# Scaling three turns deep, DMA transposes for the shared activations, accumulates moved, gathers one add sooner

## The chip, the cores and the metric

One core of a Trainium2 chip runs the whole program in one launch. The metric is the device time in microseconds, as the median of several runs. TensorE (PE) multiplies, VectorE (DVE), ScalarE (ACT) and GpSimd (POOL) do the rest, SyncE (SP) only issues DMAs and waits; GpSimd issues the indirect DMAs.

## What is computed

Two layers on `x` (16 sequences of 128 rows, 512 wide). The first is a recurrence over time (WKV) on the normalized rows and a context; the second is a mixture of eight experts, two chosen for each row, beside one shared expert:

```
x = x + wkv(w, u, layernorm(x), ctx)
h = layernorm(x)                                   # 2048 rows of 512
p = softmax(h @ gate_w.T); comb = its two largest  # 8 experts
moe = sum_e comb[:, e] * (silu(h @ eg[e].T) * (h @ eu[e].T)) @ ed[e].T      # inner size 256
sh  = (silu(h @ sg.T) * (h @ su.T)) @ sd.T         # inner size 1024
x = x + moe + sigmoid(h @ seg.T) * sh
```

## The kernel before

**Tiles.** The 2048 rows are 16 tiles of 128. The fp32 operands are split in two fp16 parts, high and low, and each product takes three matmuls (high by high, high by low, low by high). A *unit* is 256 inner columns of one tile: 12 matmuls of 512 columns into `GU` (gate and up, one of two PSUM banks), and 6 into `DN` (down). The shared expert has four units for each tile, 64 in all (`N_EXP`); behind them come 39 slots (`NSLOT`), each one unit of a gathered tile of 128 rows for one routed expert, the last slots being padding.

**One unit, n.** PE fills `GU`. ACT takes the tanh of the gate half into `th` (`unit_tanh`, L654). DVE (`hidden`) makes `th` (L1192) and then the fp32 product `hb` (L1195), and raises `h_rdy`. PE transposes `hb` in two 128x128 pieces into the PSUM bank `HT` (`hidden_t`, L829). ACT copies the high part as fp16 to `hx` (`unit_hi`, L659), DVE the low part (`hidden_lo`, L1200). Two units later PE multiplies `hx` with the down weights (`down_products`, L899). The four units of a tile add up in `DN`, which DVE adds to the tile in `accumulate` (L1206); SP stores it (`store_sum`). The order within PE's unit is: six GU matmuls, the down products of unit n - 2, HT of unit n - 1, six GU matmuls.

**Turns.** The program is written out by hand, engine by engine; each engine runs its list in order and waits on semaphores. Turn i (i = 2 to 15) does the recurrence of tile i (DVE: two scans L1061 and L1064, `add_now` L1071 which raises `nd`, four `reciprocals` L1078; ACT: `both_exps`; POOL: `first_product` L421, `second_product` L424, `quotient` L429 and L432, which gives `yb`), the residual and second norm of tile i - 1 (PE: YT from `yb`, L829; POOL: `norm`, L411 to L415; ACT: `second_norm`, `xnb`, L620; PE: XT), the routing of tile i - 2 and the four shared units of tile j = i - 2. `first_stats(i + 2)` on DVE reads the tile x(i + 2), which SP loads with `load_x`. Turns 0 and 1 have no units. After turn 15 come the last two shared tiles, while lists of rows for each expert are put together, and then the slots.

**Weights.** Each routed expert's weights are loaded (SP), squared and summed for a scale (ACT L599 in `expert_square`, PE L869 and L870 in `sum_squares`, DVE in `small_steps`, POOL in `scales`), and split: ACT makes the high parts (`expert_piece`, L702) and scaled copies (L705), POOL the low parts (`expert_lo`, L445). `SQUARED_IN` says in which turn each expert is squared; `turns` hands each engine `sq_e` (squared in this turn), `hi_e` (high parts, a turn later), `ws_e` and `lo_e`. POOL splits the shared down weights in L494.

**Slots.** POOL gathers slot j's rows (`gather_tile`, L574) into one of six buffers and adds the results with an accumulating indirect DMA (`add_rows`, L584). An add waits for `may_add`, which SP raises when the adds of earlier experts have landed; padding slots wait for all real ones. Gather 5 also waits until the last shared tile is stored.

## Time and profile before

| | us |
|---|---|
| median of 3 runs | 565.74 |
| lowest, highest | 565.31, 566.1 |
| the profiled execution | 566.06 |
| its span | 564.3 |
| granted TensorE clock, share of full speed | 0.985 |

The span runs from the first instruction to the last; the time of the execution has 1.8 us more around it. Busy times are sums of instruction durations; neighbours overlap a little, so a start-to-start distance says more than a duration. A number in brackets behind a timeline row is the idle time of the engine just before it, with what ended it.

### The profile page before, as it was taken

Reading aid. Unit: us, or ns where it says so; the run is one execution under the profiler, and the core shown is the slowest. Engines: PE = TensorE matmul, PEld = TensorE weight load, DVE = VectorE, ACT = ScalarE, POOL = GpSimd, SP = SyncE. Lnnn points to the kernel's source line nnn. Section 1 sums busy time; section 2 is a strip of 40 time slices with the busy share of each in tenths; the row PEclk is TensorE's granted clock in tenths of the full one; section 3 lists DMA queues with packets and bytes.
Section 4 is the critical chain, followed back from the end, with each engine's and each line's share of the span. In section 5 each row is a group of like instructions: output and inputs, shape, how many; then the busy total and the mean of one; then the engine's idle time right before and its main releaser. Section 6 shows DMA issues by size and latency. Waiting matters only on the chain.

```text
span 564.3 us, 10142 instructions
## 1 busy us (share of the span) xinstructions
PE 486.2 (86%) x2671; PEld 258.5 (46%) x2671; DVE 421.3 (75%) x954; ACT 275.9 (49%) x534; POOL 345.4 (61%) x422
## 2 busy tenths in 40 slices
PE   1116789899999999999999979999999999999970
PEld 1113345345455555454555435445545555555530
DVE  5678987899989899999898867566656656666650
ACT  4848837575573864765837333433333333333310
POOL 5767956857948669588486364334375565555332
PEclk9999989999999999999999999999999999999995
DMA  7970105105213223151101320315576776677453
GB/s 283 415 271 19 38 19 187 57 21 188 76 46 143 77 82 143 38 188 62 52 20 39 105 88 15 113 45 102 101 122 117 141 119 116 110 131 123 69 73 38
DMA packets 25929, 59.14 MB, mean 105 GB/s; under 512 B 6314, under 2 KB 6314, under 8 KB 24338
## 3 DMA queue, kind: packets, MB, share of 16 engines
q0 software_dynamic: 9824, 20.90, 21.3%
...
q14 instruction: 31, 0.25, 0.2%
...
## 4 chain that ended last, share of the span: by engine, by line
PE 52%; POOL 17%; issue 10%; DVE 9%; DMA 7%; ACT 3%; SPq 1%; POOLq 0%; DVEq 0%; ACTq 0%
PE GU L884 28%; PE DN L899 14%; DMA out<-wall,idsa 5%; POOL wall L445 4%; PE XT L829 3%; PE HT L829 3%; POOL yb L429 2%; POOL nrm L411 2%; POOL nrm L413 2%; DVE wall L1071 2%; POOL wall L424 2%; POOL wall L421 2%; DVE wall L1078 1%; PE YT L829 1%; SPq L366 1%
## 5 line engine op out<-in xcount | busy, mean ns | idle before, releaser
L884 PE MATMUL GU<-wall,xt 128*128 128x512 f16 x768 | 187.0, 384 | 2.1 <-DVE wall L1173 2.0
L899 PE MATMUL DN<-wall,hx 128*128 128x512 f16 (+1 forms) x618 | 150.8, 380 | 7.2 <-DVE hx L1200 4.5
L884 PEld LDWEIGHTS GU<-wall,xt 128*128 128x128 f16 x768 | 74.8, 99 | 70.4 <-issue 3.7
L584 POOL DMA_INDIRECT out<-wall,idsa x39 | 62.0, 1590 | 73.1 <-SPq L370 35.1
L659 ACT ACTIVATE hx<-HT 128x256 f16<-128x256 f32 x103 | 39.0, 379 | 127.4 <-PE HT L829 110.6
L899 PEld LDWEIGHTS DN<-wall,hx 128*128 128x128 f16 x618 | 60.4, 98 | 81.9 <-issue 6.0
L1200 DVE TENSOR_TENSOR hx<-HT,hx 128x256 f16<-128x256 f32 x103 | 43.1, 418 | 64.3 <-ACT hx L659 59.7
L654 ACT ACTIVATE th<-GU,scl 128x256 f32<-128x256 f32 x103 | 48.5, 471 | 80.0 <-PE GU L884 76.1
L884 PE MATMUL GU<-wall,kb 128*128 x240 | 61.4, 379 | 0.2 <-DVE kb L1374 0.2
L884 PE MATMUL GU<-wall,xnb 128*128 x228 | 58.5, 379 | 0.6 <-DVE xnb L1374 0.6
L574 POOL DMA_INDIRECT xb<-xn_rows,idsi x39 | 40.2, 1030 | 30.5 <-DMA out<-xb 16.3
L1078 DVE RECIPROCAL wall<-wall 128x128 f32<-128x128 f32 x64 | 57.7, 928 | 0.0
L1192 DVE SCALAR_TENSOR_TENSOR th<-th,GU 128x256 f32<-128x256 f32 x103 | 41.5, 403 | 20.5 <-ACT th L654 20.2
L1195 DVE SCALAR_TENSOR_TENSOR hb<-th,scl,GU 128x256 f32<-128x256 f32 x103 | 49.5, 481 | 9.6 <-DVE th L1192 4.8
L445 POOL TENSOR_TENSOR wall<-wall 128x1024 f16<-128x1024 f32 x21 | 44.9, 2141 | 5.4 <-ACT wall L705 3.5
L488 POOL DMA_INDIRECT lists<-toki,posi x32 | 35.4, 1107 | 13.2 <-issue 6.2
L829 PE MATMUL HT<-ident,hb 128*128 128x128 f32 x206 | 40.1, 276 | 3.3 <-DVE hb L1195 3.2
L411 POOL TENSOR_SCALAR nrm<-mv 128x1 f32<-128x1 f32 x32 | 14.1, 442 | 46.2 <-DVE mv L1086 44.7
L829 PEld LDWEIGHTS HT<-ident,hb 128*128 128x128 f32 x206 | 27.9, 141 | 26.5 <-DVE hb L1195 9.4
L1428 DVE TENSOR_SCALAR wall<-DN,scl,wsl 128x512 f32<-128x512 f32 x39 | 31.3, 802 | 2.9 <-PE DN L899 2.8
L884 PEld LDWEIGHTS GU<-wall,kb 128*128 128x128 f16 x240 | 23.5, 98 | 19.9 <-issue 0.7
L829 PE MATMUL KT<-ident,kb 128*128 128x128 f32 x64 | 11.6, 309 | 23.0 <-POOL toki L395 7.8
...
## 6 DMA issues: line engine op xcount, KB each, us to landing
...
out<-xb SPq DMA_DIRECT2D x20, 256.0 KB
xb<-x SPq DMA_DIRECT2D x16, 256.0 KB, 2.7
cb<-ctx_t SPq DMA_DIRECT2D x16, 256.0 KB
xn_rows<-xnb SPq DMA_DIRECT2D x16, 256.0 KB
xb<-xn_rows,idsi POOLq DMA_INDIRECT x39
out<-wall,idsa POOLq DMA_INDIRECT x39
```

What stands on the lines that cost most here:

```text
L445: ins = nc.gpsimd.tensor_tensor(lo, span(wall, raw, GUW // 2), hi, ALU.subtract)
L574: pool.indirect_dma_start(xg[r], None, xn_dram, bass.IndirectOffsetOnAxis(ap=idsi[:, j:j + 1], axis=0)).then_inc(gather[r], 16)
L584: pool.indirect_dma_start(out, bass.IndirectOffsetOnAxis(ap=idsa[:, j:j + 1], axis=0), ye[j % RESULTS], None, compute_op=ALU.add).then_inc ...
L654: nc.scalar.activation(th[par][:], GU[par][:, 0:IE], ACT.Tanh, scale=scale(row, TANH)).then_inc(tanh, 1)
L659: nc.scalar.activation(hx[par][:, 0:IE], HT[:, 0:IE], ACT.Copy).then_inc(h_hi, 1)
L829: ins = nc.tensor.transpose(dst[:, c * P:(c + 1) * P], src[:, c * P:(c + 1) * P], ident[:])
L884: ins = nc.tensor.matmul(GU[par][:], lhs(xp, c), gate_up(base, wp, c), start=m == 0, stop=m == 3 * HC - 1)
L899: ins = nc.tensor.matmul(DN[:], hx[par][:, hp * IE + c * P:hp * IE + (c + 1) * P], down(base, wp, c), start=start and m == 0, stop=stop an ...
L1078: nc.vector.reciprocal(a, a).then_inc(rcp, 1)
L1192: STT(th[par][:], th[par][:], 1.0, GU[par][:, 0:IE], ALU.add, ALU.mult).then_inc(a1, 1)
L1195: STT(hb[par][:], th[par][:], scale(row, KAPPA), GU[par][:, IE:2 * IE], ALU.mult, ALU.mult).then_inc(h_rdy, 1)
L1200: TT(hx[par][:, IE:2 * IE], HT[:, 0:IE], hx[par][:, 0:IE], ALU.subtract).then_inc(h_lo, 1)
```

## The change

- The constant `HX = 3`: three buffers `hx`, and the down products of unit n are issued in unit n + 3 instead of n + 2.
- For the shared units `hb` isn't transposed by PE any more. `unit_hi` and `hidden_lo` write the fp16 parts untransposed to `hr` (two buffers), and SP transposes `hr` into `hx` with one DMA (`turn_hidden`, 128x512 fp16, 128 KB, 64 of them). Every other `hb` now lies in PSUM (bank `HB`, in place of `HT`). For the slots PE still transposes, into `YT`.
- `accumulate`, `hidden_lo`, `unit_hi` and `expert_square` stand elsewhere in the lists; `load_x(i + 3)` at a turn's end becomes `load_x(i + 2)` near its start; `store_sum` is last in a turn.
- Experts are squared in the even turns 2 to 14 instead of 2, 3, 5, ..., 13, and expert 0's squares, sums and scales go into turns 2 and 3. One matmul of four columns takes the place of two of two columns. All experts get the three steps of splitting in three turns.
- An expert's weights are loaded in six DMAs of 256 KB between the transposes, instead of one of 1024 KB and one of 512 KB.
- After the turns the second norm comes ahead of expert 6's low parts on POOL, and two of these behind the read of the lists.
- Gather j is issued ahead of add j - 7 instead of behind it.

The core of the diff (in order: names, SP, POOL in turn 3, POOL after the turns and in the slots, ACT, PE):

```diff
+HX = 3
+PIECES = 6
-SQUARED_IN = [2] + list(range(3, 2 * E - 2, 2))
+SQUARED_IN = list(range(2, 2 * E, 2))
...
-        HT, DN = bank("HT"), bank("DN")
+        HB, DN = bank("HB"), bank("DN")
+        hb = [HB[:, 0:IE], hb1[:, :]]
+        hb_routed = [by_time[:, 0:IE], hb1[:, :]]
...
+            def turn_hidden(n):
+                sp.wait_ge(h_lo, n + 1)
+                wait_from(sp, dn, n - HX + 1)
+                sp.dma_start(hx[n % HX][:, :].rearrange("p (c t) -> p c t", t=P), hr[n % 2][:],
+                             transpose=True).then_inc(h_turned[n % HX], 16)
...
             def turn(i, j, sq_e, hi_e, ws_e, lo_e):
...
+                if j > 0:
+                    turn_hidden(n - 1)
...
+                if i > LAG + 1 and i + 2 < B:
+                    load_x(i + 2)
+                if i < B - 1:
+                    load_ctx(i + 1)
+                piece(0)
+                turn_hidden(n)
+                piece(1)
+                turn_hidden(n + 1)
+                store_xn(i - 1)
+                piece(2)
+                turn_hidden(n + 2)
+                if j > 0:
+                    store_sum(j - 1)
...
+                if i == LAG + 1:
+                    scales(2, 0)
...
-            expert_lo(E - 2, 1)
-            expert_lo(E - 2, 2)
             norm(B - 1, 1, agg2, norm2, xn_rdy)
+            expert_lo(E - 2, 0)
...
+            expert_lo(E - 2, 1)
+            expert_lo(E - 2, 2)
             scales(E + 1, E - 1)
...
                 gather_tile(j)
-                add_rows(j - GATHERS)
+                if j > GATHERS:
+                    add_rows(j - GATHERS - 1)
...
             def unit_hi(n, par):        
-                act.wait_ge(h_t, n + 1)
-                wait_from(act, dn, n - 1)
-                nc.scalar.activation(hx[par][:, 0:IE], HT[:, 0:IE], ACT.Copy).then_inc(h_hi, 1)
+                act.wait_ge(h_rdy, n + 1)
+                if n >= 2:
+                    act.wait_ge(h_turned[(n - 2) % HX], 16 * ((n - 2) // HX + 1))
+                nc.scalar.activation(hr[par][:, 0:IE], hb[par], ACT.Copy).then_inc(h_hi, 1)
...
                 second_norm(i - 1)
+                unit_hi(n + 1, 1)
...
                 if i + 1 < B:
                     both_exps(i + 1)
-                unit_hi(n + 1, 1)
...
                 if before is not None:
-                    down_products(n - 2, par, *before)
-                if not (isinstance(n, int) and n == 0):
-                    hidden_t(n - 1, 1 - par)
+                    down_products(n - HX, *before)
+                if n > N_EXP:
+                    hidden_t(n - 1)
...
-            down_products(n - 2, n % 2, base_of[NSLOT - 2], True, True, B + NSLOT - 2)
-            hidden_t(n - 1, (n - 1) % 2)
-            down_products(n - 1, (n - 1) % 2, base_of[NSLOT - 1], True, True, B + NSLOT - 1)
+            hidden_t(N_EXP + NSLOT - 1)
+            for j in range(NSLOT - HX, NSLOT):
+                down_products(N_EXP + j, base_of[j], True, True, B + j)
```

VectorE in one turn, before, from the low part of unit n - 1 (the previous tile's last) to `hidden` of unit n + 2:

```order
277 L1200 TENSOR_TENSOR hx<-HT,hx 128x256
278 L1071 TENSOR_TENSOR wall<-wall 128x8x127
...
286 L1081 BN_STATS st<-xb 128x6
287 L1086 BN_AGGR mv<-st 128x2
288 L1200 TENSOR_TENSOR hx<-HT,hx 128x256
289 L1206 SCALAR_TENSOR_TENSOR xb<-DN,gate,xb 128x512
290 L1078 RECIPROCAL wall<-wall 128x128
...
294 L1078 RECIPROCAL wall<-wall 128x128 x2
295 L1200 TENSOR_TENSOR hx<-HT,hx 128x256
296 L1078 RECIPROCAL wall<-wall 128x128
```

and the same place afterwards (L1263 is `hidden_lo`, L1131 `add_now`, L1269 `accumulate`, L1138 a reciprocal, L1141 the statistics):

```order
320 L1263 TENSOR_TENSOR hr<-hb,hr 128x256
321 L1131 TENSOR_TENSOR wall<-wall 128x8x127
...
329 L1263 TENSOR_TENSOR hr<-HB,hr 128x256
330 L1141 BN_STATS st<-xb 128x6
331 L1146 BN_AGGR mv<-st 128x2
332 L1138 RECIPROCAL wall<-wall 128x128
...
336 L1138 RECIPROCAL wall<-wall 128x128
337 L1269 SCALAR_TENSOR_TENSOR xb<-DN,gate,xb 128x512
338 L1138 RECIPROCAL wall<-wall 128x128
339 L1263 TENSOR_TENSOR hr<-hb,hr 128x256
340 L1138 RECIPROCAL wall<-wall 128x128
```

The low part of unit n moved ahead of the statistics of the next x, and the accumulate moved from there to between the reciprocals, behind `hidden` of unit n + 1.

SP in one turn with weights, before (L275 `load_x`, L280 `load_ctx`, L284 `store_xn`, L290 `store_sum`):

```order
56 L280 DMA cb<-ctx_t 128x512
57 L305 DMA wall<-wgu 128x2048
58 L306 DMA wall<-wd 128x1024
59 L284 DMA xn_rows<-xnb 128x512
60 L290 DMA out<-xb 128x512
```

and afterwards (L282 `load_x`, L320 `turn_hidden`, L314 a piece of weights):

```order
60 L320 DMA_TRANSPOSE hx<-hr 128x4x128
61 L282 DMA xb<-x 128x512
62 L287 DMA cb<-ctx_t 128x512
63 L314 DMA wall<-wgu 128x512
64 L320 DMA_TRANSPOSE hx<-hr 128x4x128
65 L314 DMA wall<-wgu 128x512
66 L320 DMA_TRANSPOSE hx<-hr 128x4x128
67 L291 DMA xn_rows<-xnb 128x512
68 L314 DMA wall<-wgu 128x512
69 L320 DMA_TRANSPOSE hx<-hr 128x4x128
70 L297 DMA out<-xb 128x512
```

Four transposing DMAs stand between SP's others, each behind a wait for its own unit's low part; the load of x is ahead of the reading turn's other transfers and behind one of them.

## Rows read from the trace of the kernel before

**Rows 1.** The page: busy us (share of the span), instructions of each engine.
```profile
PE 486.2 (86%) x2671; PEld 258.5 (46%) x2671; DVE 421.3 (75%) x954; ACT 275.9 (49%) x534; POOL 345.4 (61%) x422
```
**Rows 2.** Busy time by stretch; columns in the header, counts in brackets.
```profile
core 0: us, PE busy (x) PEld busy (x) DVE busy (x) ACT busy (x) POOL busy (x), PEclk, DMA share, GB/s
...
73.00:318.00 245.00, 237.75 (x1372) 125.47 (x1370) 221.30 (x515) 149.81 (x301) 171.78 (x231) 0.99 0.25 85
...
363.00:543.00 180.00, 177.68 (x934) 95.95 (x932) 110.48 (x234) 56.11 (x116) 92.60 (x70) 1.00 0.60 105
```
**Rows 3.** The same view of one pair of turns.
```profile
199.23:237.02 37.79, 36.95 (x217) 19.88 (x216) 35.24 (x83) 23.84 (x48) 27.88 (x37) 1.00 0.27 98
```
**Rows 4.** Timeline of TensorE in that pair: start, duration, instruction.
```profile
207.99 0.38 PE L829 MATMUL HT<-ident,hb 128*128 128x128 f32 x2
208.21 1.46 PE L884 MATMUL GU<-wall,xt 128*128 128x512 f16 x6
...
228.68 0.66 PE L829 MATMUL YT<-ident,yb 128*128 128x128 f32 x4 [0.84 <-POOL yb L432]
```
**Rows 5.** Timeline of VectorE in the same pair.
```profile
213.36 0.42 DVE L1200 TENSOR_TENSOR hx<-HT,hx 128x256 f16<-128x256 f32 x1
213.70 1.21 DVE L1071 TENSOR_TENSOR wall<-wall 128x1016 f32<-128x1016 f32 x1
...
217.51 0.67 DVE L1081 BATCH_NORM_STATS2 st<-xb 128x6 f32<-128x512 f32 x1
...
223.97 0.42 DVE L1200 TENSOR_TENSOR hx<-HT,hx 128x256 f16<-128x256 f32 x1 [0.68 <-ACT hx L659]
...
228.61 0.42 DVE L1200 TENSOR_TENSOR hx<-HT,hx 128x256 f16<-128x256 f32 x1
```
**Rows 6.** Timeline of GpSimd in the same pair: the end of its chain.
```profile
228.35 0.27 POOL L432 TENSOR_SCALAR yb<-cb 128x4 f32<-128x4 f32 x1
```
**Rows 7.** Table of DMA issues: KB each, median us to landing.
```profile
xb<-x SPq DMA_DIRECT2D x16, 256.0 KB, 2.7
```
**Rows 8.** Timeline of SP's issues in the same pair.
```profile
205.52 0.33 SPq L275 DMA_DIRECT2D xb<-x  x1
...
210.19 0.42 SPq L306 DMA_DIRECT2D wall<-wd  x1
```
**Rows 9.** Timeline of ScalarE in turn 2.
```profile
55.22 1.04 ACT L599 ACTIVATE junk<-wall 128x1024 bf16<-128x1024 f32 x1
```
**Rows 10.** The chain that ended last, in turn 2: start, us, what.
```profile
66.22 2.04 issue
68.26 1.27 POOL wall L421
```
**Rows 11.** Timeline of TensorE: three of its waits.
```profile
100.34 1.47 PE L899 MATMUL DN<-wall,hx 128*128 128x512 f16 x6 [0.91 <-DVE hx L1200]
...
330.58 0.66 PE L829 MATMUL XT<-ident,xnb 128*128 128x128 f32 x4 [3.19 <-ACT xnb L620]
...
355.91 1.46 PE L899 MATMUL DN<-wall,hx 128*128 128x512 f16 x6 [1.00 <-DVE xb L1206]
```
**Rows 12.** The page's groups: GpSimd's low parts of experts.
```profile
L445 POOL TENSOR_TENSOR wall<-wall 128x1024 f16<-128x1024 f32 x21 | 44.9, 2141 | 5.4 <-ACT wall L705 3.5
```
**Rows 13.** Timeline of GpSimd in the slots: gather 5, add 5, gather 12, adds 36 and 37.
```profile
375.79 2.54 POOL L574 DMA_INDIRECT xb<-xn_rows,idsi  x1 [14.78 <-DMA out<-xb]
...
410.22 1.59 POOL L584 DMA_INDIRECT out<-wall,idsa  x1 [4.59 <-DVE wsl L1439]
412.12 0.99 POOL L574 DMA_INDIRECT xb<-xn_rows,idsi  x1 [0.30 <-SPq L370]
...
544.27 1.56 POOL L584 DMA_INDIRECT out<-wall,idsa  x1 [2.88 <-DVE wall L1428]
552.11 1.56 POOL L584 DMA_INDIRECT out<-wall,idsa  x1 [6.28 <-SPq L370]
```
**Rows 14.** Timeline of VectorE at the end: the result of slot 36, and the last `hb`.
```profile
543.18 0.81 DVE L1428 TENSOR_SCALAR wall<-DN,scl,wsl 128x512 f32<-128x512 f32 x1
...
544.55 0.48 DVE L1195 SCALAR_TENSOR_TENSOR hb<-th,scl,GU 128x256 f32<-128x256 f32 x1 [0.17 <-DVE th L1192]
```

192 lines of the change are left out of this document (112 added, 80 removed).

## The prediction

> **What bounds the kernel now.** I read the page first, then the idle time of TensorE, then one pair of turns on every engine. The page gives TensorE 86% of the span and VectorE 75% [rows 1], an average over five stages; the table by stretch separates two of them [rows 2]. Turns 3 to 15 fill 73 to 318 us: TensorE is busy 237.8 us of 245, but VectorE is busy 221.3. The routed stage, 363 to 543 us, is TensorE's alone (177.7 of 180). Before 73 us ScalarE, VectorE and GpSimd wait for one another in turn 2, and behind the last slot there are transfers and waits.
>
> Two turns repeat with a period of 37.8 us, of which TensorE is busy 36.95 and VectorE 35.24 [rows 3]. So each turn costs 18.9 us, and an engine stands right behind TensorE. What ends TensorE's idle time here is the transpose YT, which waits 0.84 us for GpSimd's `yb` in one turn of two [rows 4]. GpSimd's chain in that turn runs from 214.8 us, where VectorE has made the sums (`nd`) that it waits for, to 228.6 us: two scatters, two products of L445, two norms, two products, the quotient [rows 5, 6]. VectorE waits about 2.0 us in the pair, nearly all of it before three of its eight `hx` rows, for ScalarE; one of them is the 0.68 us at 223.97 [rows 5]. Its work, with the small gaps between instructions, therefore needs about 35.8 us per pair.
>
> **The transposes that go.** Each shared unit loses its two TensorE transposes HT. From one start to the next, two of them take 208.21 - 207.99 = 0.22 us [rows 4]; their busy time of 0.38 overlaps the neighbours. Per pair of turns that is 8 units x 0.22 = 1.76 us. The second sum-of-squares matmul, which takes its place in the stream for as long (0.2 us), goes once per pair, since one matmul of four columns takes the place of both. TensorE's own work is 37.8 - 0.84 = 36.96 us now, so about 35.0 us afterwards.
>
> But GpSimd's chain is untouched by that: from its start to `yb` it keeps its 13.8 us, while the units ahead of YT shrink by three transposes, 0.66 us. The wait of 0.84 becomes 1.5 us in the turn with the two L445 products. TensorE's side of the pair is then 35.0 + 1.5 = 36.5 us.
>
> **VectorE's side.** `hidden_lo` still runs eight times per pair, reading `hb` instead of HT. Its present step is 213.70 - 213.36 = 0.34 us [rows 5]; half of them now read SBUF alone, for which I take off 0.2 us per pair in all. The rest is the same work in another order. The waits for ScalarE that followed HT mostly go, because `unit_hi` starts on `h_rdy` and stands ahead of the four exponentials. So 35.6 us, plus what the change adds: `load_x(i+2)` is now issued in the same turn that reads it, behind `turn_hidden(n-1)`. From the end of `hidden_lo(n-1)` (213.78) to `first_stats(i+2)` (217.51, plus 0.35 for the `hidden_lo` placed ahead) VectorE has 4.1 us; such a load takes 2.7 us from issue to landing [rows 5, 7]. That leaves about 1.3 us for issuing the transposing DMA. A plain DMA occupies SP for 0.33 to 0.42 us [rows 8], the bound below; no row shows the transposing form, and with 2.6 us as the bound above the wait would be 1.3 us per turn. I take 0.3 us, nearer the plain issue: 35.6 + 0.6 = 36.2 us.
>
> The larger side sets the pair: 36.5 us against 37.8, so 1.3 us. In 245 us there are 6.5 pairs: **-8.5 us**, with ends of -18 (TensorE's 35.0 alone) and +3 (VectorE with 1.3 us a turn: 35.6 + 2.6 = 38.2).
>
> **The turned activations.** The 64 DMAs of 128 KB have to land in time. From the end of `hidden_lo` to the down products there are, by units of 4.4 us and a lag of three, 6.7, 5.7, 5.7 and 5.7 us for the four units of a turn: for instance the `hidden_lo` of the third unit stands at 228.61 and ends at 229.0 [rows 5], and its products would come one unit and six GU matmuls behind the YT of 228.68 [rows 4], at about 234.7. The nearest row is a plain transfer of 256 KB with 2.7 us [rows 7]; on the other side stands an accumulating scatter, 544.27 until it releases the next at 552.11, less SP's bookkeeping in between: about 4.8 us [rows 13]. I take 3 to 4.5 us with queueing behind a 256 KB piece, which is under 5.7: cost nothing, cover the two units of matmuls between. Beyond 5.7 us both TensorE (operand) and ScalarE (`hr` is overwritten two units later) wait, and the loop closes over three units, so each us costs a third of a us per unit. SP's other waits in a turn (`xn_rdy`, `dn_free`, `y_rdy`) stand behind the transposing DMA that is due earlier, and those events are past by then.
>
> What the Trainium skill says here, apart from the sum: "VectorE: DVE Perf Modes", section "The three transpose paths", gives 1309 ns for one 128x128 tile by DMA against 390 ns on TensorE and advises TensorE where PSUM will do. Four tiles one after the other would be an estimated 5.2 us by that page of the Trainium skill, at the very edge of the window, which speaks against the change. "Advanced Engine Details and Errata", section "X-Bar Transpose (TRN2)", says instead that transposing DMAs are as fast as others, an estimated 0.4 us of transfer. No run shown here decides between the two; for TensorE the trace gives 0.11 us each in the stream, below the 390 ns of the Trainium skill [rows 4].
>
> **Start.** In turn 2, ScalarE loses the three squares of expert 0 (three of some 1.1 us, the first at 55.22) [rows 9]. GpSimd waited for the exponentials behind them, 66.22 to 68.26 [rows 10], so YT(2) comes 2.0 us sooner; GpSimd's own work up to 66.2 is then next. Turn 3 gains the squares instead: TensorE waits behind unit 1 for the third square, which follows a tanh on ScalarE (0.5 + 1.15 us), +1.7, and `scales(2, 0)` ahead of `first_product(4)` costs YT(3) some 0.6. Expert 0's pieces 4 and 5 leave turn 3 (2 x 1.1 us), where they had pushed `hx` and `hb`: TensorE's wait of 0.91 us at 100.34 [rows 11] and the two of 0.8 us that follow it within six us mostly go, -2.2. Sum **-1.9 us**, ends -5 and +3.
>
> **After the turns.** GpSimd did two L445 products, 2.14 us each [rows 12], ahead of `norm(B - 1)`; TensorE waited 3.19 us for `xnb`, until 330.58 [rows 11]. With the norm first `xnb` can be there up to 4.3 us sooner, before TensorE arrives: -3.2. The wait of 1.00 us at 355.91 for the accumulate goes [rows 11], since that is placed a unit later, with the products it needs: -1.0. HT in eight units is 1.8 us, of which the chain of lists may eat half: -0.8. Here `expert_lo(E-2, 1)` and `(2)` and `scales` follow the read of the lists, 4.3 + 2.6 us on GpSimd, which then idled nearly as long for the lists to come back, so the first gather stays about where it was. Sum **-5.0 us**, ends -6 and -1.
>
> **Routed stage.** Its transposes stay, in YT, so 39 slots keep 4.54 us. The gathers come one slot sooner in the row and the adds one slot later. At its head, `accumulate(B - 1)` moves from slot 1 to 2, and gather 5, which waits for its store (375.79 now) [rows 13], slips by 4.5 us to about 380.3; it lands at the 384 us where unit 4 wants it: +0.7. The wait of 1.3 us for gather 12, queued behind add 5 (410.22, 412.12) [rows 13], goes: -1.3. Sum **-0.5 us**, ends -2 and +3.
>
> **End.** A lag of three leaves `down(36)` behind the last unit. Slot 36's result was written at 543.18 and added at 544.27; the two slots after it wait for that add to land, the next goes at 552.11 [rows 13, 14]. With the change: last `hb` 545.0 [rows 14], HT's two transposes, six matmuls 1.3, the result 0.8, the add issued at 547.6: **+3.3 us**, nothing covers it.
>
> **Sum.** -8.5 - 1.9 - 5.0 - 0.5 + 3.3 = -12.6 us. The profiled execution took 566.06 us around its span of 564.3; the median is 565.74. From 566.06 that gives 553.5, and against the median 553.1. I say **553.2 us**.
>
> **Rivals.** *Late turns, slower.* If the transposing DMA takes over 5.7 us, or occupies SP longer than a unit, every turn pays: 4/3 us per turn for each us of excess, over 16 sets. The gain of 12.6 is used up at an excess of 0.6, landing in 6.3 us; at 7 us the time is 553.2 + 16 x 1.7 = 581. For it: there is no row of its kind, and one in-order queue shared with loads. Against: plain transfers of twice the size land in 2.7. The 1309 ns per tile of the Trainium skill ("VectorE: DVE Perf Modes", "The three transpose paths") would lead here if the issue and a piece of weights came on top; no run shown bears it out. Chance 0.18.
> *VectorE waits for x.* With 1.3 us a turn the turns cost 38.2 us per pair and the gain there turns into +3: 564.5, no change to speak of. For it: the load was a whole turn ahead before. Chance 0.14.
> *TensorE alone.* The GpSimd wait does not grow, for its chain starts sooner with VectorE ahead: 35.0 to 35.4 us per pair, -17: 545. Chance 0.12.
> *As forecast*, 547 to 560: 0.56.
>
> About 0.2%, 1.1 us, is what a measurement of this kernel can tell from no change. Faster holds the forecast, TensorE alone and half of the x rival, 0.75; same 0.06; slower 0.19, the late turns and a little of the x rival. The range takes in the x rival and TensorE alone and leaves out the far half of the late turns: 543 to 569.
>
> **What would show it.** Right: a pair of turns of about 36.5 us, YT waiting 1.5 us for `yb` in one turn of two, no wait before DN for the DMA, no wait before `xnb` at 320 us, and slots of 4.54 us. Wrong: DN or `hr` waiting for the DMA transposes, SP busy over 1.3 us in one, VectorE idle before the statistics of x, or YT without a wait at all.

## The result and the profile after

The kernel after takes 576.19 us (median of four runs, 575.17 to 577.17) against 565.57 us for the kernel before beside it (565.31 to 566.1): a ratio of 1.0181 with a 95% interval of 1.0144 to 1.0217. It is slower by 10.6 us where 12.6 us less were forecast, and lies outside the range. The profiled span is 573.4 us, 9.1 more than before.

The page of the kernel after, to be held against [rows 1]: TensorE is busy 10.1 us less than before and VectorE 8.9 us more; the wait of YT for `yb`, 30.7 us, heads TensorE's idle time.

```profile
PE 476.1 (83%) x2525; PEld 242.0 (42%) x2525; DVE 430.2 (75%) x954; ACT 274.3 (48%) x534; POOL 345.9 (60%) x422
L886 PE MATMUL YT<-ident,yb 128*128 128x128 f32 x64 | 11.8, 314 | 30.7 <-POOL yb L475 30.7
```

Marks on TensorE's timeline (the router products of turns 5 and 15, the transposes of slot 0's gathered tile, the start of the last unit's gate-up products, the end) cut the 9.1 us into pieces. For each I set the forecast beside it; the -8.5 us of the pairs is spread by 1.3 us a pair, since one pair lies ahead of turn 5 and half a pair behind turn 15:

| stretch | before, us | after, us | change | forecast |
|---|---|---|---|---|
| start to turn 5 (119.53, 118.94) | 119.5 | 118.9 | -0.6 | -1.9 and -1.3 |
| ten turns, 5 to 15 | 188.65 | 190.76 | +2.1 | -6.5 |
| turn 15 to the first slot | 53.34 | 57.09 | +3.75 | -5.0 and -0.7 |
| slots | 177.51 | 177.83 | +0.3 | -0.5 |
| end | 25.3 | 28.8 | +3.5 | +3.3 |

**The pair of turns.** The table by stretch for one pair from router to router answers to [rows 3]: the pair is 37.57 us long where it was 37.8; TensorE is busy 35.20 us of it (35.0 forecast), VectorE 35.91 (35.24 before), and VectorE waits 1.1 us besides, 0.47 of it for x.

```profile
196.89:234.46 37.57, 35.20 (x200) 17.54 (x198) 35.91 (x83) 23.54 (x48) 28.05 (x38) 1.00 0.50 129
```

TensorE's timeline, YT alone: first the kernel before, then after. The number in brackets is the wait ahead of it. What TensorE no longer does stands there as waiting: 2.07 + 0.30 us a pair, where it was 0.84.

```profile
190.88 0.66 PE L829 MATMUL YT<-ident,yb 128*128 128x128 f32 x4 [0.84 <-POOL yb L432]
209.50 0.60 PE L829 MATMUL YT<-ident,yb 128*128 128x128 f32 x4
228.68 0.66 PE L829 MATMUL YT<-ident,yb 128*128 128x128 f32 x4 [0.84 <-POOL yb L432]
```
```profile
192.51 0.66 PE L886 MATMUL YT<-ident,yb 128*128 128x128 f32 x4 [0.29 <-POOL yb L475]
212.09 0.66 PE L886 MATMUL YT<-ident,yb 128*128 128x128 f32 x4 [2.07 <-POOL yb L475]
230.08 0.66 PE L886 MATMUL YT<-ident,yb 128*128 128x128 f32 x4 [0.30 <-POOL yb L475]
```

GpSimd in the turn between the first two of these YT, kernel after (other lines left out). From the end of one `yb` (192.45) to the next (212.04) there are 19.6 us, and no bracket in it is above 0.52: scales, two scatters, two low parts of weights (L488), two norms, two products, the quotient, back to back.

```profile
192.22 0.23 POOL L475 TENSOR_SCALAR yb<-cb 128x4 f32<-128x4 f32 x1
...
198.62 1.14 POOL L531 DMA_INDIRECT lists<-toki,posi  x1 [0.52 <-POOL scl L520]
...
201.06 2.13 POOL L488 TENSOR_TENSOR wall<-wall 128x1024 f16<-128x1024 f32 x1
...
204.49 2.13 POOL L488 TENSOR_TENSOR wall<-wall 128x1024 f16<-128x1024 f32 x1
...
211.79 0.25 POOL L475 TENSOR_SCALAR yb<-cb 128x4 f32<-128x4 f32 x1
```

The same turn of the kernel before, from the `yb` at 209.07 to the one at 228.35 [rows 6]. GpSimd has no gap here either; its longest wait is about a third of a us:

```profile
209.07 0.23 POOL L432 TENSOR_SCALAR yb<-cb 128x4 f32<-128x4 f32 x1
...
215.25 1.13 POOL L488 DMA_INDIRECT lists<-toki,posi  x1 [0.29 <-DVE mask L1166]
...
217.66 2.14 POOL L445 TENSOR_TENSOR wall<-wall 128x1024 f16<-128x1024 f32 x1
...
221.09 2.13 POOL L445 TENSOR_TENSOR wall<-wall 128x1024 f16<-128x1024 f32 x1
```

**Behind the turns.** GpSimd, VectorE and TensorE of the kernel after around the read of the lists. GpSimd's two low parts stand where the change put them, behind the read; a 24-element subtract on VectorE that starts 0.20 us ahead of them takes 4.46 us and ends with them (in the kernel before it took 0.18); the cast of the ids stands behind it on VectorE, so TensorE waits 4.39 us, and 12 products behind the wait take 4.45 us where others take 2.75.

```profile
348.35 4.22 POOL L488 TENSOR_TENSOR wall<-wall 128x1024 f16<-128x1024 f32 x2
```
```profile
348.15 4.46 DVE L1372 TENSOR_TENSOR cb<-lga,mxa 128x24 f32<-128x24 f32 x1
...
356.82 0.26 DVE L1470 CAST yb<-by_time 39x128 f32<-39x128 int32 x1
```
```profile
357.13 0.25 PE L1066 MATMUL KT<-ident,yb 39*128 39x39 f32 x1 [4.39 <-DVE yb L1470]
357.32 4.45 PE L940 MATMUL GU<-wall,xt 128*128 128x512 f16 x12
...
362.90 2.75 PE L940 MATMUL GU<-wall,xt 128*128 128x512 f16 x12
```

ScalarE at the end of turn 15: all six pieces of expert 6 stand ahead of the norm `xnb` that TensorE then waits 2.64 us for (3.19 before, [rows 11]). In the kernel before two pieces stood there (2.17 us from 322.91).

```profile
322.97 3.21 ACT L754 ACTIVATE wall<-wall,scl 128x1024 f16<-128x1024 f32 x3
326.09 3.21 ACT L757 ACTIVATE wall<-wall,scl 128x1024 f32<-128x1024 f32 x3
...
329.51 0.80 ACT L665 ACTIVATE xnb<-xb,nrm 128x512 f32<-128x512 f32 x1
```

**The transposing DMAs.** The view of the tile `hx` on SP's queue: 64 issues, each 1.2 us of SP. In this kernel TensorE waited for one of them only: the products 0.2 us, their weight load 0.7. That DMA was issued at 347.42, so it took 3.85 us from the start of its issue to the weight load at 351.27.

```profile
L320 SPq DMA_TRANSPOSE hx<-hr x64: 1189/1196/1601, 58.1 to 372.2; - x64
...
who waited for it (us, times):
  PEld DN L958: 0.7, 1
  PE DN L958: 0.2, 1
```
```profile
351.27 0.33 PEld L958 LDWEIGHTS DN<-wall,hx 128*128 128x128 f16 x3 [0.67 <-DMA hx<-hr]
```

### The profile page after: what moved, and what is told of

Same layout as the page of the kernel before. It is cut to its first block, busy times and chain, and to the rows that moved or that the text cites. A ratio compares the mean times of both kernels' runs of the same rounds, so it can differ in the third digit from the quotient of the medians.

```text
span 573.4 us, 9946 instructions
## 1 busy us (share of the span) xinstructions
PE 476.1 (83%) x2525; PEld 242.0 (42%) x2525; DVE 430.2 (75%) x954; ACT 274.3 (48%) x534; POOL 345.9 (60%) x422
## 2 busy tenths in 40 slices
DMA packets 65353, 67.53 MB, mean 118 GB/s; under 512 B 41642, under 2 KB 41642, under 8 KB 64786
## 4 chain that ended last, share of the span: by engine, by line
PE 37%; POOL 18%; DVE 17%; issue 11%; DMA 7%; ACT 4%; SPq 3%; POOLq 0%; DVEq 0%; ACTq 0%
PE GU L940 21%; PE DN L958 11%; DVE wall L1138 4%; POOL wall L488 3%; PE XT L886 3%; DMA out<-wall,cb 3%; POOL yb L472 2%; PE YT L886 2%; POOL nrm L454 2%; DMA xb<-x 2%; POOL wall L467 2%; POOL nrm L456 2%; DVE st L1141 1%; POOL wall L464 1%; DMA xb<-xn_rows,cb 1%
## 5 line engine op out<-in xcount | busy, mean ns | idle before, releaser
L940 PE MATMUL GU<-wall,xt 128*128 128x512 f16 x768 | 191.6, 392 | 4.5 <-DVE wall L1233 4.5
L628 POOL DMA_INDIRECT out<-wall,cb x39 | 62.0, 1589 | 73.5 <-SPq L413 35.9
L1138 DVE RECIPROCAL wall<-wall 128x128 f32<-128x128 f32 x64 | 59.1, 932 | 0.0
L618 POOL DMA_INDIRECT xb<-xn_rows,cb x39 | 38.6, 989 | 33.8 <-DMA out<-xb 21.5
L1261 DVE TENSOR_TENSOR hx<-YT,hx 128x256 f16<-128x256 f32 x39 | 16.5, 424 | 40.8 <-ACT hx L706 40.8
L488 POOL TENSOR_TENSOR wall<-wall 128x1024 f16<-128x1024 f32 x21 | 44.8, 2135 | 0.2
L706 ACT ACTIVATE hx<-YT 128x256 f16<-128x256 f32 x39 | 14.9, 383 | 61.4 <-PE YT L886 61.4
L886 PE MATMUL YT<-ident,yb 128*128 128x128 f32 x64 | 11.8, 314 | 30.7 <-POOL yb L475 30.7
L1494 DVE TENSOR_SCALAR wall<-DN,scl,cb 128x512 f32<-128x512 f32 x39 | 31.3, 803 | 4.9 <-PE DN L958 4.6
L940 PEld LDWEIGHTS GU<-wall,xnb 128*128 128x128 f16 x228 | 22.3, 98 | 18.8 <-issue 0.7
L1141 DVE BATCH_NORM_STATS2 st<-xb 128x6 f32<-128x512 f32 x32 | 22.1, 692 | 8.1 <-DMA xb<-x 7.5
```

Source lines behind the costliest of these rows:

```text
L488: ins = nc.gpsimd.tensor_tensor(lo, span(wall, raw, GUW // 2), hi, ALU.subtract)
L618: pool.indirect_dma_start(xg[r], None, xn_dram, bass.IndirectOffsetOnAxis(ap=idsi[:, j:j + 1], axis=0)).then_inc(gather[r], 16)
L628: pool.indirect_dma_start(out, bass.IndirectOffsetOnAxis(ap=idsa[:, j:j + 1], axis=0), ye[j % RESULTS], None, compute_op=ALU.add).then_inc ...
L886: ins = nc.tensor.transpose(dst[:, c * P:(c + 1) * P], src[:, c * P:(c + 1) * P], ident[:])
L940: ins = nc.tensor.matmul(GU[par][:], lhs(xp, c), gate_up(base, wp, c), start=m == 0, stop=m == 3 * HC - 1)
L1138: nc.vector.reciprocal(a, a).then_inc(rcp, 1)
```

## The experiments

The theory after this reading (theory A in what follows): in the turns of the kernel after, a loop through GpSimd, with ScalarE and VectorE in it, sets the time, not TensorE; behind the turns, three placements cost time each in its own place. The rivals: TensorE still bounds the pair; the transposing DMAs cost something themselves; VectorE alone bounds.

**1. Give TensorE its work back.** In `unit`, ahead of the products:

```diff
+                if 0 < n <= N_EXP:
+                    for c in range(IC):
+                        nc.tensor.transpose(GU[par][:, c * P:(c + 1) * P], ident[:], ident[:])
                 products(par, lhs, base, 0, 3)
```

> The kernel after, with two 128x128 transposes of the identity ahead of each unit's gate-up products in the turns and the first unit of the slots (64 units), so that TensorE has back about the work that the change took from it (2 x 0.11 to 0.14 us a unit, near 2 us a pair of turns, 15 to 18 us over the whole), while the DMA transposes stay. Results are unchanged. Theory A (in the steady turns TensorE is not the bound; its freed time became the wait for yb): the filling goes into the waits, 0 to +3 us, so 576 to 579 us, and the YT waits shrink from 30.7 us to about 16. Rival (TensorE's own work bounds the pair): +12 to +15 us, 588 to 591. Third: if the shorter idle time gives the clock back, it could even come out 1 to 3 us faster than the kernel after.

Measured: 579.09 us, 1.0233 [1.0198, 1.0268], 2.9 us above the kernel after. The pair is 38.3 us instead of 37.6, though 1.6 us of work went in (TensorE busy 36.81 us for 35.20), so TensorE did not bound it. But it stands close behind: 0.7 of the 1.6 us lengthened the pair, and the waits of YT fell to 24.4 us in all, not to the 16 that theory A gave.

```profile
212.72 0.66 PE L886 MATMUL YT<-ident,yb 128*128 128x128 f32 x4 [1.47 <-POOL yb L475]
```

**2. The moves without the DMAs.** `hb` in SBUF, transposed by TensorE into a bank, `unit_hi` and `hidden_lo` reading the bank; all positions, the distance of three units and the tail as in the kernel after:

```diff
-                if n > N_EXP:
+                if n > 0:
                     hidden_t(n - 1)
-                act.wait_ge(h_rdy, n + 1)
-                nc.scalar.activation(hr[par][:, 0:IE], hb[par], ACT.Copy).then_inc(h_hi, 1)
+                act.wait_ge(h_t, n + 1)
+                nc.scalar.activation(hx[n % HX][:, 0:IE], HB[:, 0:IE], ACT.Copy).then_inc(h_hi, 1)
```

> The kernel after with everything that it moves kept, but the shared units' hidden activations transposed by TensorE into a PSUM bank as before (two 128x128 transposes a unit, behind the down products of unit n-3) and no transposing DMA. It splits the change into the transposes and the moves. Theory A (the moves made the rest of the loss, the DMA transposes gained nothing because TensorE was not the bound): within 2 us of the kernel after, 575 to 579 us. Rival B (the transposing DMAs themselves cost, by queue or memory): it goes back towards 565 to 570. Rival C (the DMA transposes gained their TensorE time and the moves lost far more): 588 and above.

Measured: 576.86 us, 1.0214 [1.0176, 1.0252]; theory A. In the table by stretch (columns as in [rows 3]) its pair is 38.05 us, TensorE busy 36.91, so the DMAs bring 0.5 us of the 1.8 a pair; turn 3 gave that back, for its router stood at 77.0 us here and at 80.5 in the kernel after (run 12 looks at that). From turn 15 to the first slot it is the other way round, 60.5 us here and 57.1 there. With the DMAs or without, the moves cost the 10.6 us.

```profile
192.82:230.87 38.05, 36.91 (x216) 19.65 (x215) 35.25 (x83) 23.88 (x48) 27.66 (x38) 1.00 0.34 98
```

**3. and 4. GpSimd less, VectorE less,** in the kernel after:

```diff
+                if k == 1 and e < E - 2:
+                    nc.gpsimd.memset(lo, 0.0)
+                    return
                 ins = nc.gpsimd.tensor_tensor(lo, span(wall, raw, GUW // 2), hi, ALU.subtract)
```
```diff
-                    nc.vector.reciprocal(a, a).then_inc(rcp, 1)
+                    nc.vector.reciprocal(a[:, 0:T // 2], a[:, 0:T // 2]).then_inc(rcp, 1)
```

> The kernel after with GpSimd's second low-part subtraction of experts 0 to 5 (128x1024, 2.135 us each, one a pair of turns) replaced by a memset of the same half-width region; the routed experts' low parts of that half are left out of the computation, nothing else changes. GpSimd gets 1 to 2 us a pair. Theory A (the pair closes over a loop through GpSimd, ScalarE and VectorE, and GpSimd's share is on it): each pair gets shorter by 1 to 2 us, 5 to 11 us in all, 565 to 571. Rival B (VectorE alone bounds the pair): little, 0 to 2 us. If a memset on GpSimd takes as long as the subtraction, this says nothing.

> The kernel after with the reciprocals (64 of 128x128, 0.932 us each, four a turn) over the first 64 columns only, which leaves half of each quotient's reciprocal out of the computation; VectorE gets about 0.4 us each, 1.7 us a turn, 3.4 us a pair back. Theory A (loop through GpSimd, ScalarE and VectorE, with VectorE's queue on it in the even turn): the pair falls from 37.6 towards TensorE's own 35.0 plus its waits, 1.5 to 2.5 us a pair, 10 to 16 us in all, 560 to 566. Rival (GpSimd alone bounds): 0 to 3 us.

Measured: 569.64 us, 1.0083 [1.0057, 1.0108], and 565.81 us, 0.9995 [0.9978, 1.0011]. The totals look as if VectorE were worth more; the pair says otherwise. GpSimd's 1.17 us less (the memset takes 0.965 us) made the pair 36.53 (190.24 to 226.77), 1.04 us shorter; VectorE's 3.2 us less made it 37.24 (186.90 to 224.14), 0.33 shorter. So nine tenths of what GpSimd lost came off the pair. Of VectorE's it was one tenth, or three tenths of what its busy time lost: that fell by 1.07 us only (34.84 for 35.91), as small operations beside GpSimd's grew longer (the two of 128x16 in a pair from 1.02 to 2.14 us).

Run 4's total doesn't measure VectorE. Of the 9.2 us by which its span is shorter, 2.1 lie ahead of turn 5 and 3.0 in the ten turns. The other 4.1 lie behind the turns, 3.2 of them behind the last down products, where no reciprocal stands and only the waits between the last adds changed. The values left out go into the routing, so the lists of rows can differ; that this is the reason is inferred. First run 3, then run 4:

```profile
190.24 0.66 PE L889 MATMUL YT<-ident,yb 128*128 128x128 f32 x4 [0.29 <-POOL yb L475]
208.84 0.66 PE L889 MATMUL YT<-ident,yb 128*128 128x128 f32 x4 [1.14 <-POOL yb L475]
226.77 0.66 PE L889 MATMUL YT<-ident,yb 128*128 128x128 f32 x4 [0.25 <-POOL yb L475]
```
```profile
206.41 0.66 PE L886 MATMUL YT<-ident,yb 128*128 128x128 f32 x4 [2.05 <-POOL yb L475]
```

**5. The low parts ahead of the read of the lists,** in GpSimd's tail:

```diff
             scatter(B - 4)
-            for t in range(B - 3, B):
+            scatter(B - 3)
+            expert_lo(E - 2, 1)
+            expert_lo(E - 2, 2)
+            for t in range(B - 2, B):
                 scatter(t)
...
-            expert_lo(E - 2, 1)
-            expert_lo(E - 2, 2)
             scales(E + 1, E - 1)
```

> The kernel after with GpSimd's last two low-part subtractions of expert 6 (2 x 2.1 us) back ahead of the read of the lists (between the second and the third of the last four scatters) instead of behind it. Theory A (in the kernel after they run beside VectorE's 24-element subtract at 348.15, which takes 4.46 us until they end, and TensorE then waits 4.39 us for the slots' ids and falls to half clock for 1.7 us more): the 4.46 us subtract falls to 0.2 us, the ids' transpose comes up to 4.4 us sooner and no clock is lost, -4.4 to -6 us, 570 to 572. Rival (the list read itself, now 2 to 4 us later, is what TensorE waits for): 0 to -2 us, and the subtract is short all the same.

Measured: 568.38 us, 1.0053 [1.0033, 1.0073], 7.8 us less than the kernel after: the largest single placement, and more than the 4.4 to 6 expected. By the profiles the span is 7.1 us shorter: 5.9 in the stretch of the edit, turn 15 to the first slot (51.17 for 57.09), and 0.7 in the ten turns, where the edit changes nothing. The subtract is short again, and the wait for the ids and the slow products behind it are gone:

```profile
347.33 0.18 DVE L1373 TENSOR_TENSOR cb<-lga,mxa 128x24 f32<-128x24 f32 x1
```

**6. ScalarE's last pieces out of turn 15,** on top of run 5:

```diff
-                if i == B - 1:
-                    ws_e = hi_e
...
             unit_hi(n, 0)
+            expert_piece(E - 2, 4)
+            expert_piece(E - 2, 5)
             router_out(B - 1)
```

> The same as the one before (GpSimd's two subtractions ahead of the read of the lists), and ScalarE's last two scaled pieces of expert 6 (2 x 1.1 us) out of turn 15, where the change had put them ahead of the norm for which TensorE waits, to behind the first hidden copy that follows the turns. Theory A (TensorE's 2.64 us for xnb at 330.37 is ScalarE's queue of six pieces): the wait falls by 1.6 to 2.6 us and the half clock behind it (1.3 us) goes, -1.6 to -3 us against the run before, 567 to 570. Rival (the norm waits for GpSimd anyway, or the pieces come back as a wait of GpSimd's low parts): 0, and GpSimd's read of the lists later.

Measured: 569.93 us, 1.0085 [1.0052, 1.0118], 1.6 us above run 5 with intervals that overlap: the rival. TensorE's wait for `xnb` halved, from 2.65 to 1.32 us, but a wait of 4.00 us for VectorE's `posi` came in its place. It is the same collision again: a 16-column operation of VectorE on SBUF alone takes 3.84 us until GpSimd's two low parts are done.

```profile
334.60 4.21 POOL L488 TENSOR_TENSOR wall<-wall 128x1024 f16<-128x1024 f32 x2
```
```profile
335.01 3.84 DVE L1198 TENSOR_TENSOR pos<-ones,pos 128x16 f32<-128x16 f32 x1
```
```profile
339.84 0.17 PE L934 MATMUL LG<-mask,tri 128*128 128x8 f16 x1 [4.00 <-DVE posi L1218]
```

**7. The end in the order of before.** On the kernel after:

```diff
+            down_products(N_EXP + NSLOT - HX, base_of[NSLOT - HX], True, True, B + NSLOT - HX)
             hidden_t(N_EXP + NSLOT - 1)
-            for j in range(NSLOT - HX, NSLOT):
+            for j in range(NSLOT - HX + 1, NSLOT):
```

with VectorE's `expert_rows(NSLOT - HX)` likewise ahead of the last `hidden_lo`.

> The kernel after with only the end in the order of before: the third-last slot's down product ahead of the last slot's transposes, and its rows ahead of the last low part, so that its add starts sooner. Theory A (the end is a chain of adds that starts when the third-last slot's rows are ready, and the change pushed that row back by the last transposes and their 1.78 us wait): -2.0 to -3.3 us, 573 to 574. Rival (the adds are bound by the last one's own row): 0.

Measured: 572.96 us, 1.0139 [1.0102, 1.0177]. Of the 3.2 us the trace shows 1.1 at the end (from the last gate-up products at 545.76 to the end of the span, 24.8 us; 26.0 in the kernel after). The rest is in the turns, where this profile lacks the slow groups that the one of the kernel after has at 173.34. The interval overlaps that of the kernel after.

**8. The load of x ahead of the transposing DMA,** in SP's turn:

```diff
+                if i > LAG + 1 and i + 2 < B:
+                    load_x(i + 2)
                 if j > 0:
                     turn_hidden(n - 1)
                 if i == LAG:
                     load_x(i + 3)
-                if i > LAG + 1 and i + 2 < B:
-                    load_x(i + 2)
```

> The kernel after with the load of the turn's rows of x issued by SP ahead of the turn's first transposing DMA instead of behind it. Theory A (VectorE's waits for x, 0.47 us in the odd turns and 2.9 us over all turns, are time at which it holds the loop): -1 to -3 us, 573 to 575. Rival (VectorE makes the wait up because GpSimd is later anyway): within 1 us of 576.

Measured: 573.66 us, 1.0152 [1.0115, 1.0189], 2.5 us less by the medians, but again with overlapping intervals and the same steady pair of 37.6 us. That the load costs anything is not shown.

**9. and 10. The three repairs together (5, 7 and 8), with the DMAs and without** (the latter with the edit of run 2):

> The kernel after with three of the repairs together: GpSimd's two subtractions ahead of the read of the lists, the end in the order of before, and the loads of x ahead of the turn's first transposing DMA. Theory A (the three are independent, since they lie in three stretches): 576.2 - 7.8 - 3.2 - 2.5 = 562.7 us, 561.5 to 564.5, below the kernel before. Rival (a part of each gain was the clock's or a later stage takes it back): 565 to 568.

> The same three repairs, and the shared units' hidden activations transposed by TensorE as before, without the transposing DMAs. It shows what the transposing DMAs are worth when the other moves no longer hide it. Theory A (nothing in the turns, since the pair closes over GpSimd, ScalarE and VectorE; the steady pair was 38.05 us with TensorE's transposes and 37.6 with the DMAs, 2.7 us over six pairs, and turn 2 gave that back): 562 to 565 us, within 1.5 us of the run before. Rival (they are worth their 2.7 us or more now): 565 to 567.

Measured: 565.98 us, 1.0004 [0.9987, 1.0020], and 569.55 us, 1.0057 [1.0036, 1.0078]. The first is 3.3 us above the sum of the parts, as could be said of 7 and 8 above: their medians promised more than their rows. The second is slower by 3.6 us with intervals apart: the transposing DMAs do bring something once the other stretches hide nothing. The profiles, each of the longest execution of its kernel, are 5.1 us apart: 1.2 ahead of turn 5, 0.5 in the ten turns (0.5 a pair, less a slow group of 1.7 that only run 9 has there), 2.5 between turn 15 and the first slot, and 0.9 behind. In run 9 a longer wait stands in the slots: 2.02 us for a gathered tile, with slow products behind it.

```profile
383.54 0.65 PE L887 MATMUL XT<-ident,xb 128*128 128x128 f32 x4 [2.02 <-DMA xb<-xn_rows,cb]
...
385.19 2.63 PE L959 MATMUL DN<-wall,hx 128*128 x6
```

**11. Two units behind in the slots.** On the kernel after with the edits of 5 and 8, the down products at a distance of two in the slots, as before; `accumulate(B - 1)` so comes one slot sooner:

```diff
-                if j == HX - 1:
+                if j == 1:
                     accumulate(B - 1)
-                if j >= HX:
-                    expert_rows(j - HX)
+                if j >= 2:
+                    expert_rows(j - 2)
```

> The kernel after with GpSimd's two subtractions ahead of the read of the lists and the load of x ahead of the transposing DMA (two of the three repairs that gave 566.0 together), and in the slots the down products two units behind instead of three, as before: the last mix tile's accumulate stands one slot sooner, and the end drains two units. Theory A (the three-unit distance holds the last tile's accumulate, store and so the sixth gather back, for which TensorE waits 2.0 us and drops to half clock, and it lengthens the end): 566.0 less 2 to 4 us, 562 to 564. Rival (the end alone matters, and its repair already gave that): 565.5 to 566.5.

Measured: 563.27 us, 0.9958 [0.9943, 0.9974]: 2.1 us less than the kernel before, and 2.7 us less than run 9, intervals apart. VectorE's accumulate moves from 376.03 to 372.41 us (first run 9, then this one), and the gathered tile for which run 9 waited 2.02 us no longer comes late.

```profile
376.03 0.74 DVE L1271 SCALAR_TENSOR_TENSOR xb<-DN,gate,xb 128x512 f32<-128x512 f32 x1
```
```profile
372.41 0.74 DVE L1273 SCALAR_TENSOR_TENSOR xb<-DN,gate,xb 128x512 f32<-128x512 f32 x1
```

**12. VectorE's scans behind `yb` in turn 3,** on the kernel after:

```diff
+                if i == LAG + 1:
+                    dve.wait_ge(y_rdy, i)
                 scan_e(i)
                 scan_ev(i)
```

> The kernel after with one wait added: in turn 3 VectorE's two scans wait for the yb of turn 2. In the kernel after they start at 70.84, beside GpSimd's product of yb at 70.91, which takes 2.23 + 1.02 us there and 1.29 + 0.23 us where nothing runs beside it (the kernel with TensorE's transposes), and one of the scans takes 2.25 us instead of 1.2. Theory A (they hold each other up): the yb product ends 1.7 us sooner, TensorE's wait of 7.16 us falls to 5.4, and turn 3 starts 1 to 1.7 us sooner: 574.5 to 575.2 us. Rival (VectorE, 1.6 us later, gives it back in turn 3): 576.

Measured: 573.87 us, 1.0138 [1.0095, 1.0180], an interval that overlaps that of the kernel after. The rows are clear. In the kernel after `yb` took 2.23 + 1.02 us beside the scans:

```profile
70.91 2.23 POOL L472 TENSOR_TENSOR yb<-wall 128x512 f32<-128x512 f32 x1
73.23 1.02 POOL L475 TENSOR_SCALAR yb<-cb 128x4 f32<-128x4 f32 x1
```

and here, with VectorE held, 1.29 + 0.24; YT comes at 72.37 us and not at 74.31, turn 3's router at 78.96 and not at 80.51:

```profile
70.70 1.29 POOL L472 TENSOR_TENSOR yb<-wall 128x512 f32<-128x512 f32 x1
72.08 0.24 POOL L475 TENSOR_SCALAR yb<-cb 128x4 f32<-128x4 f32 x1
```

**13. and 14. The kernel before, two of the moves alone.** The last norm ahead of expert 6's low parts (these between the scatters, as in run 5) and `accumulate(B - 2)` ahead of its neighbour unit; then the gathers one add sooner as well (GpSimd's part of the first is shown):

```diff
-            expert_lo(E - 2, 1)
-            expert_lo(E - 2, 2)
             norm(B - 1, 1, agg2, norm2, xn_rdy)
             scatter(B - 4)
-            for t in range(B - 3, B):
+            scatter(B - 3)
+            expert_lo(E - 2, 1)
+            expert_lo(E - 2, 2)
+            for t in range(B - 2, B):
                 scatter(t)
```

> The kernel before with two of the change's moves alone: the last turn's norm ahead of GpSimd's last two low parts of expert 6, which then go between the second and the third of the last scatters, and the accumulate of the second-last tile ahead of its neighbour unit. Theory A (before, TensorE waits 3.19 us for xnb at 330.58 and 1.00 us at 355.91 for DN, and both go): -3.2 to -4.2 us, 561.4 to 562.5. Rival (as in the kernel after, ScalarE's queue is next, and the wait shrinks by a fraction): 0 to -1.5 us, 564 to 565.6.

> The same on the kernel before, and the gathers of the slots issued one add sooner. Theory A (TensorE waits about 1.3 us at one slot for a gathered tile): a further -1.0 to -1.5 us. Rival (an issue earlier on one queue pushes the adds back by the same, and the end is the adds'): 0 to +1 us.

Measured: 561.26 us, 0.9926 [0.9898, 0.9953], and 560.75 us, 0.9915 [0.9887, 0.9942], the fastest version here that computes everything, ahead of both kernels. The wait for `xnb` fell from 3.19 us to 0.38 and the one for DN went: without ScalarE's four further pieces in the way the two moves give nearly what the prediction gave them. Turn 15 to the first slot became 2.8 us shorter (50.50 for 53.34). A new wait of 1.48 us for `posi` took part of it back, behind a 128x16 operation of VectorE of 1.55 us that ends with GpSimd's two low parts, the collision of run 6 once more. Of the 5.1 us between the two profiles another 1.5 lies ahead of turn 5, where the edit changes nothing. The gathers alone add 0.5 us, which the intervals don't tell from nothing.

```profile
326.21 0.66 PE L830 MATMUL XT<-ident,xnb 128*128 128x128 f32 x4 [0.38 <-ACT xnb L621]
```

**15. and 16. Did TensorE bound the pair of before?** The edits of 3 and 4, on the kernel before.

> The kernel before with GpSimd's second low-part subtraction of experts 0 to 5 (2.1 us each) replaced by a memset of the same region, so that half's low parts are left out of the computation. In the kernel after the same edit gave GpSimd 1.17 us a pair (2.135 to 0.965) and shortened the pair by 1.05 us (37.6 to 36.5). It asks whether TensorE bounded the pair of before, as the prediction took it. If TensorE does (own work 36.96 of 37.8): the wait for yb of 0.84 us goes at most, 0 to 0.85 us a pair, 0 to -5 us in all, and the pair ends near 37.0. If the loop through GpSimd bounds it already: -1.05 a pair, 36.8, -6.5 us in all.

> The kernel before with the reciprocals over half their columns (half of each quotient left out of the computation): VectorE gets 0.4 us on each of 64, 3.2 us a pair. In the kernel after the same edit moved the steady pair by 0.35 us only, and the whole by 10.4 us, most of it at the start and behind the turns. If TensorE and the loop through GpSimd bound the pair of before: 0 to -0.5 us a pair, and little at the start and the end, where TensorE's own waits are shorter: -2 to -5 us, 561 to 564. If VectorE bounds it: -1 us a pair and more, below 558.

Measured: 566.34 us, 1.0013 [0.9990, 1.0036], and 558.76 us, 0.9898 [0.9857, 0.9940]. Ten turns took 188.7 us before, 188.1 with less GpSimd work (117.7 to 305.8) and 187.9 with less VectorE work (116.2 to 304.1). On the average neither frees the pair. With GpSimd shorter, the wait for `yb` is gone (first row below). In the pair around 207 us the turn that ended in it fell from 19.18 to 18.32 us from YT to YT, by just that wait; the other turn rose from 18.62 to 19.03. With VectorE shorter, three of the five pairs came to 36.7 us, TensorE's own work without idle time, and the other two to 38.9 and 39.0 (the two rows by stretch, columns as in [rows 3], are one of each). So TensorE's own 36.7 to 37.0 us is the floor under the pair, and the other engines stand close behind it. That TensorE alone bounded the pair as it stood is not shown: its one wait was for GpSimd. Run 16's total has the same flaw as run 4's, 3.1 us of it lie in the end.

```profile
207.61 0.66 PE L832 MATMUL YT<-ident,yb 128*128 128x128 f32 x4
```
```profile
116.16:152.83 36.67, 36.67 (x217) 20.04 (x216) 31.61 (x81) 23.50 (x47) 26.46 (x37) 1.00 0.30 102
152.83:191.76 38.93, 37.27 (x217) 19.53 (x216) 33.24 (x84) 24.40 (x50) 28.01 (x37) 1.00 0.28 96
```

**17. and 18. Move GpSimd's work into its idle time.** In both lines, the first two low parts of an expert at the front of the turn in which GpSimd idles for 5 us, and ScalarE's fifth piece a turn sooner. On run 11 with the edit of run 12, and on run 14 (GpSimd's part of the first is shown):

```diff
-                if lo_e is not None:
-                    expert_lo(lo_e, 1)
+                if ws_e is not None:
+                    expert_lo(ws_e, 0)
+                    expert_lo(ws_e, 1)
```

> The kernel with two of the repairs and the two-unit distance in the slots (563.3 us), with the wait ahead of turn 3's scans, and with GpSimd's first two low-part subtractions of an expert (2 x 2.14 us) moved to the front of the even turn, where GpSimd stands idle for 5.0 us before the norm (212.0 to 217.1 in the steady pair); for it ScalarE makes the fifth scaled piece one turn sooner, in a gap of 1.7 us. All work stays. The odd turn, where TensorE waits 2.09 us for yb, has one subtraction instead of two. Theory A (the loop through GpSimd bounds the pair at about one for one, VectorE at a tenth, TensorE's own work is 35.0 to 35.3 us): -1.5 to -2.1 us a pair over six pairs and -1.5 at turn 3, 549 to 553 us. Rival B (VectorE's 35.8 us and ScalarE's latency stand right behind): -0.5 to -1 a pair, 556 to 559. Rival C (nothing, since the work comes back as waits elsewhere): 561 to 563.

> The same move of GpSimd's subtractions, and of ScalarE's fifth piece, on the best version of the kernel before (560.75 us: norm and accumulate sooner, gathers one add sooner). Its difference from the run above is what the transposing DMAs and the change's other moves are worth once GpSimd is off the loop. Theory A (TensorE's own 36.96 us bounds the pair of before, which stands at 37.8): the wait for yb of 0.84 us a pair goes at most, -2 to -5 us, 556 to 559, so the kernel after, so repaired, is the faster by 3 to 8 us. Rival (the pair of before is bound by GpSimd as much): below 555.

Measured: 564.87 us, 0.9974 [0.9959, 0.9989], and 565.61 us, 0.9996 [0.9979, 1.0012]: nothing on the first, 4.9 us lost on the second. The turn that waited 2.07 us for `yb` did become 2.0 us shorter (router to router 196.05 to 213.64, 17.6 us, against 19.6), for the 2.14 us that left it. The other became 2.5 us longer (20.54 against 17.99). I had put the two behind GpSimd's wait for the mask, so that they did not fill the idle time but began at its end and pushed the norm back:

```profile
217.15 4.23 POOL L488 TENSOR_TENSOR wall<-wall 128x1024 f16<-128x1024 f32 x2 [4.43 <-DVE mask L1228]
```

What they give ahead of that wait was not tried, so whether the 549 to 553 us of that expectation can be had stays open.

## Why the prediction was wrong

Two steps failed: the pair of turns, 8.6 us off over the ten turns, and the stretch behind the turns, 9.4 us off.

**The pair, -8.5 us.** TensorE's own work came out as worked out (35.20 us against 35.0). What failed is the sentence that let the wait grow from 0.84 to 1.5 us, "from its start to `yb`" GpSimd "keeps its 13.8 us". It took VectorE's `nd` as the start. The trace names `mask`, and GpSimd hardly waited for it (0.29 us): in the kernel before, too, it worked from the `yb` of one turn (209.30) to that of the next (228.62) almost without a gap, 19.3 us, of the 19.2 from YT to YT. That turn was GpSimd's already. Taking work from TensorE in it could only lengthen the wait; the turn became 19.6. Only the other turn, 18.6 long with no wait, had something to give, and came to 18.0. So 0.2 us a pair, not 1.3. Runs 1, 2, 3 and 15 show it from four sides. On top, the ten turns hold a pair with a group at half clock and a longer first pair, about 1.9 and 0.9 us: that is the +2.1.

VectorE's side was no bound, but its work was misjudged as well: 0.67 us more in the pair, where the step took 0.2 off. The largest part is in small operations beside GpSimd's (the two of `chosen`, 128x2, take 1.28 us for 0.33).

The rival *TensorE alone* is refuted: the pair is 37.6 us, not 35.0 to 35.4. *Late turns* was given 0.18 and had the right sign, for a wrong reason: the DMAs landed in time but for 0.2 us, as the step on the turned activations had it, and the landing that can be read, 3.85 us, lies in its 3 to 4.5 and between the 0.4 and the 5.2 that stand beside it. *VectorE waits for x* did not happen: it waited 2.9 us over all the turns, less than the 0.3 a turn in the sum, though SP was held 1.2 us by each transposing DMA, three times the plain issue to which I had set it near; run 8 could not show that it costs time.

**Start, -1.9, and one pair, -1.3.** Measured -0.6 at turn 5. Turn 3 gained its wait for the squares as said (1.60 us), but YT(2) did not come 2.0 us sooner: it came 2.0 later, 74.31 for 72.35. The 2.0 sooner were never there. The step read "66.22 2.04 issue" [rows 10] as GpSimd waiting, but GpSimd's timeline has two low parts of the shared weights running until its first product at 68.26:

```profile
64.09 4.21 POOL L494 TENSOR_TENSOR wall<-wall 128x1024 f16<-128x1024 f32 x2
```

The 2.0 later are a collision: VectorE, free sooner, ran its scans beside GpSimd's `yb`, and both slowed down (run 12 gives 1.9 us of it back at YT and 1.55 at the router).

**After the turns, -5.0, and half a pair, -0.7.** Measured +3.75. The accumulate's 1.0 us did go. Of the 3.19 us for `xnb` only 0.55 went: the step looked at GpSimd's queue and not at ScalarE's, on which the same change put four more pieces ahead of the norm, six for two; on the kernel before, where they aren't, 2.8 went (run 13). And "GpSimd idled nearly as long for the lists to come back" costed the two low parts at nothing, naming their cover on GpSimd alone. GpSimd did have the time; what they cost was VectorE's next small operation, 4.3 us, with the cast behind it, TensorE's 4.39 us of waiting and 1.7 more for the clock: run 5 gave back 5.9 us in this stretch.

**Slots and end.** +0.3 for -0.5, since TensorE waited twice for gathers: 0.87 us at gather 5, as said, and still 1.15 us at 427.17, a slot later than the wait of 1.3 that was to go. And +3.5 for +3.3, where the chain of row, add and bookkeeping was worked out by its steps. The add came 0.5 us later than by these (9.1 us behind the start of the last unit, for 8.6), its landing 0.3 us sooner.

**The clock.** No term had it. Behind some of the long waits the products run at half clock, 1.2 for 2.4 GHz, for some 2 to 5 us. Over the groups of products that take longer than 0.24 us each, the excess is about 9.2 us after and 3.8 before. Where it happens a wait costs TensorE 1.5 to 1.7 us again, as at 172.84, 330.37 and 357.13 us; behind the waits of 2.07 to 2.32 us at 134.53, 212.09, 249.92 and 287.49 it cost nothing. Here is the one in the steady turns, with the granted clock of its stretch by the view of stretches, 0.60:

```profile
172.84 0.66 PE L886 MATMUL YT<-ident,yb 128*128 128x128 f32 x4 [2.06 <-POOL yb L475]
173.34 2.47 PE L940 MATMUL GU<-wall,xt 128*128 128x512 f16 x6
175.60 2.17 PE L958 MATMUL DN<-wall,hx 128*128 128x512 f16 x6
```
```profile
173.34:177.62 4.28, 4.28 (x15) 1.56 (x13) 4.25 (x7) 2.42 (x4) 1.99 (x2) 0.60 0.35 97
```

Three repairs of placement (runs 5, 8 and 11) bring the changed kernel to 563.3 us; its DMA transposes are then worth about 3.6 us (runs 9 and 10), a third of the 11.4 us that 1.76 us a pair over 6.5 pairs would be. Three of the moves on the old kernel bring it to 560.75 (run 14). Why the repaired kernel after (run 11) still stands 2.5 us above that was not settled. By the profiles, whose spans are 3.8 us apart, it is 0.7 us longer to turn 5, 1.0 in the ten turns, 0.9 from there to the first slot and 1.5 in the slots, and 0.4 shorter in the end.
